# RWKV block with a feed-forward branch: chunks taken in pairs, the up projection by Strassen's algorithm

## What is computed

```python
def attn(x):                      # RWKV v4
    shifted = pad(x, one token)[:, :-1]
    r, k, v = ((mu * x + (1 - mu) * shifted) @ W.T for mu, W in ((mu_r, Wr), (mu_k, Wk), (mu_v, Wv)))
    wkv = wkv_v4(k, v, w, u)      # a recurrence over the tokens: max, exponentials, sums
    return (sigmoid(r) * wkv) @ Wo.T

def ffn(x):
    hidden = silu(x @ W1.T) * (x @ W3.T)       # 2048 wide: the up projection
    return fwht(hidden) @ W2.T                 # Walsh-Hadamard transform, then down

xn = layernorm(x)
out = x + attn(xn) + ffn(xn)
```

## Time and profile before

| | |
|---|---|
| median of 3 runs | 2851.76 us (2851.28 to 2851.79) |
| the profiled execution, its own time | 2851.35 us |
| its span in the trace | 2849.5 us |
| PE, busy share of the span | 99% |
| PEld, busy share | 81% |
| DVE, busy share | 71% |
| ACT, busy share | 32% |
| POOL, busy share | 3% |
| HBM traffic | 191 GB/s over the span |

### The profile page before, as it was taken

How to read it: one execution, slowest core, us unless ns; L and a number is a source line. 1 busy time by engine, 2 the same in 40 slices (tenths; PEclk the granted TensorE clock), 3 DMA queues, 4 the chain that set the end, 5 groups by cost and what they waited for, 6 DMA issues and landing times.

```text
span 2849.5 us, 36275 instructions
## 1 busy us (share of the span) xinstructions
PE 2823.4 (99%) x12352; PEld 2318.1 (81%) x12352; DVE 2014.9 (71%) x2888; ACT 921.1 (32%) x1571; POOL 97.8 (3%) x70
## 2 busy tenths in 40 slices
PE   7999999999999999999999999999999999999999
PEld 4778888888888888888888888888888888888887
DVE  5796767767677775767757677676776767767575
ACT  5444242242322324223242332423224242242321
POOL 0450000000000000000000000000000000000000
PEclk9999999999999999999999999999999999999999
DMA  9777555455555655546455555554545555464554
GB/s 349 248 253 273 185 170 200 163 201 178 185 184 169 207 170 187 193 165 205 162 200 183 174 194 169 191 184 170 200 168 198 178 185 187 165 212 167 172 171 148
DMA packets 168930, 545.97 MB, mean 192 GB/s; under 512 B 20416, under 2 KB 20544, under 8 KB 166464
## 3 DMA queue, kind: packets, MB, share of 16 engines
q1 hardware_dynamic: 168896, 545.53, 56.4%
HBM read 492.97 MB, written 52.49 MB: 191 GB/s over the span
## 4 chain that ended last, share of the span: by engine, by line
PE 96%; DVE 2%; DMA 1%; ACT 0%; issue 0%; POOL 0%; SPq 0%; ACTq 0%; DVEq 0%
PE bank L481 16%; PE bank L483 16%; PE bank L482 16%; PE acc L498 10%; PE acc L497 10%; PE acc L496 10%; PE bank L458 6%; PE bank L457 6%; PE bank L459 6%; PE acc L542 1%; PE acc L519 0%; DMA raw<-units_w 0%; DMA raw<-units_r 0%; DMA fly<-units_w 0%; DVE pab L773 0%; DMA xrow<-x 0%
## 5 line engine op out<-in xcount | busy, mean ns | idle before, releaser
L481 PE MATMUL bank<-xs,ring 128*128 128x512 f32 x1564 | 609.3, 390 | 2.5 <-POOL ring L420 2.4
L483 PE MATMUL bank<-xs,ring 128*128 128x512 f32 x1564 | 608.5, 389 | 0.0
L482 PE MATMUL bank<-xs,ring 128*128 128x512 f32 x1564 | 608.5, 389 | 0.0
L496 PE MATMUL acc<-ring,hid 128*128 128x512 f32 x1024 | 398.4, 389 | 0.4 <-POOL ring L420 0.4
L498 PE MATMUL acc<-ring,hid 128*128 128x512 f32 x1024 | 398.8, 389 | 0.0
L497 PE MATMUL acc<-ring,hid 128*128 128x512 f32 x1024 | 398.3, 389 | 0.0
L859 DVE SCALAR_TENSOR_TENSOR hidf<-hidf,bank 128x512 f32<-128x512 f32 x256 | 175.6, 686 | 284.0 <-ACT hidf L630 284.0
L641 ACT ACTIVATE hid<-hidf 128x512 fp32r<-128x512 f32 x256 | 162.1, 633 | 659.3 <-DVE hidf L862 659.3
L481 PEld LDWEIGHTS bank<-xs,ring 128*128 128x128 f32 x1564 | 293.6, 188 | 65.6 <-DVE hidf L862 3.0
L483 PEld LDWEIGHTS bank<-xs,ring 128*128 128x128 f32 x1564 | 293.6, 188 | 61.0
L482 PEld LDWEIGHTS bank<-xs,ring 128*128 128x128 f32 x1564 | 293.5, 188 | 61.1 <-issue 0.2
(11 more groups left out here) (94 smaller groups left out, 4046.9 us busy)
## 6 DMA issues: line engine op xcount, KB each, us to landing
ring<-split_units SPq DMA_DIRECT2D x780, 512.0 KB, 3.3
split_units<-ring SPq DMA_DIRECT2D x60, 512.0 KB, 4.1
xt<-x_t SPq DMA_DIRECT2D x16, 1024.0 KB, 7.9
res<-x SPq DMA_DIRECT2D x16, 1024.0 KB, 6.4
xrow<-x SPq DMA_DIRECT2D x15, 1024.0 KB, 5.3
out<-res SPq DMA_DIRECT2D x15, 1024.0 KB, 6.0
mix<-token_rows SPq DMA_DIRECT2D x16, 512.0 KB, 4.2
raw<-units_w SPq DMA_DIRECT2D x32, 256.0 KB, 4.6
```

The source lines that it names most:

```text
L481: pe.matmul(banks[b + n][:, :], w[:, 0, col], xs[:, 0, kt, :], start=kt == 0, stop=False)
L482: pe.matmul(banks[b + n][:, :], w[:, 1, col], xs[:, 0, kt, :], start=False, stop=False)
L483: last = pe.matmul(banks[b + n][:, :], w[:, 0, col], xs[:, 1, kt, :], start=False, stop=kt == KT - 1)
L496: pe.matmul(acc[tt][:, :], a[:, 0, col], w[:, 0, :], start=first, stop=False)
```

## The change

Chunks are taken in pairs, 512 tokens (a) and the next 512 (b). For an inner tile the up projection of a pair is a product of 2 x 2 blocks: gate and linear part (W1, W3) by the two halves of the 512 channels, times the two halves of the channels by a and b. Instead of eight block products of 6 matmuls it makes seven (`product`), from sums of the weight halves (`make_sums`, by POOL, once) and sums of the x halves (`right_made` and `right_lo` on DVE, `right_hi` on ACT, once a pair). The seven results are put together in four PSUM banks and in SBUF. ACT copies four intermediate sums out of PSUM in each inner tile (`copy_sum`), and DVE adds three times.

The hidden tiles of a go to the down projection in the same step; PE spreads the four token tiles of one down unit over the seven products. The hidden tiles of b are stored to DRAM (`spilled`), and are loaded again, split and multiplied after the last inner tile (`down_b`), with the k, v and r units of the next pair in turn between them (`r_unit`). No weight unit is resident; W2 and Wo units are loaded twice in a pair.

The recurrence has eight items in a pair (one in the previous down phase, six in the up phase, one after it). Of the five DVE instructions that made the arguments of the exponentials two are left: DVE makes two differences, ACT takes Relu of them and of their negatives, 128 x 1024 each, and then the exponentials, 128 x 1024 each (`rectified`, `exponentials`). Four other DVE instructions of 128 x 512 become two of 128 x 1024.

All units are split by ACT (high) and POOL (low). In the first pair POOL also makes the sums.

```diff
-CHUNKS = B * T // N
+PAIRS = B * T // (2 * N)
+PIECES = (1, 2, 6, 5, 7, 3, 4)
+LEFT_AT = {1: (0, 0), 2: (0, 1), 6: (1, 0), 5: (1, 1), 7: (2, 0), 3: (2, 1), 4: (3, 0)}
+RIGHT = {1: 0, 2: 1, 6: 2, 5: 3, 7: 4, 3: 5, 4: 6}
+WO_AT = {5: 1, 8: 2, 10: 3}
...
+            def make_sums(j):
+                w1, w3 = (raw[RAW_AT[name, j] % RAW] for name in ("w1", "w3"))
+                near, far = slice(0, C // 2), slice(C // 2, C)
+                wait_raw(pool, ("w1", j))
+                wait_raw(pool, ("w3", j))
+                if j == 0:
+                    pool.wait_ge(w2_psum, 2 * FT)
+                else:
+                    pool.wait_ge(split_lo, SPLIT_AT["u", j - 1, 2] + 1)
+                pool.tensor_tensor(sums[:, 1, :], w3[:, near], w3[:, far], ALU.add).then_inc(sum_made, 1)
+                pool.tensor_tensor(sums[:, 2, :], w1[:, near], w3[:, near], ALU.subtract).then_inc(sum_made, 1)
+                pool.wait_ge(sum_made, 4 * j + 1)
+                pool.tensor_tensor(sums[:, 0, :], sums[:, 1, :], w1[:, near], ALU.subtract).then_inc(sum_made, 1)
+                pool.wait_ge(sum_made, 4 * j + 3)
+                pool.tensor_tensor(sums[:, 3, :], w1[:, far], sums[:, 0, :], ALU.subtract).then_inc(sum_made, 1)
...
+            def product(s, j, piece):
+                i, half_unit = LEFT_AT[piece]
+                bank = alpha if piece == 2 else gamma[(j + 2) % 3] if piece in (5, 3) else gamma[j % 3]
+                fresh = piece in (1, 2, 5)
+                w = up_weights(s, j, i)
+                if piece == 1:
+                    if j == 0:
+                        wait(pe, xs_hi, s, 7)
+                        wait(pe, xs_lo, s, 7)
+                        wait(pe, kvr_ready, s, R_UNITS - 3)
+                    elif j == 1:
+                        wait(pe, kvr_ready, s, R_UNITS)
+                    else:
+                        wait(pe, gate_b_sum, s, j - 1)
+                elif piece == 2:
+                    if j == 0:
+                        wait(pe, kvr_ready, s, R_UNITS - 2)
+                    else:
+                        wait(pe, gate_a_sum, s, j)
+                elif piece == 5:
+                    if j == 0:
+                        wait(pe, kvr_ready, s, R_UNITS - 1)
+                    else:
+                        wait(pe, ha_full, s, j)
+                else:
+                    wait(pe, u_copied, s, 4 * j + {6: 1, 7: 2, 3: 3, 4: 4}[piece])
+                for kt in range(2):
+                    at = half_unit * 2 * P + kt * P
+                    col = slice(at, at + P)
+                    high, low = (a[:, RIGHT[piece], kt, :] for a in (xs_high, xs_low))
+                    pe.matmul(bank[:, :], w[:, 0, col], high, start=fresh and kt == 0, stop=False,
+                              skip_group_check=True)
+                    pe.matmul(bank[:, :], w[:, 1, col], high, start=False, stop=False, skip_group_check=True)
+                    last = pe.matmul(bank[:, :], w[:, 0, col], low, start=False, stop=kt == 1,
+                                     skip_group_check=True)
+                last.then_inc(u_done, 1)
...
+            def up_step(s, j):
+                i = SPREAD_AT.get(j)
+                product(s, j, 1)
+                product(s, j, 2)
+                if i is not None:
+                    down_a(s, i, (0,))
+                product(s, j, 6)
+                product(s, j, 5)
+                if i is not None:
+                    down_a(s, i, (1,))
+                product(s, j, 7)
+                product(s, j, 3)
+                if i is not None:
+                    down_a(s, i, (2,))
+                product(s, j, 4)
+                if i is not None:
+                    down_a(s, i, (3,))
+                if j in EXTRA_AT:
+                    down_a(s, EXTRA_AT[j], range(TT))
...
+            def pair(s):
+                for j in range(FT):
+                    up_step(s, j)
+                down_a(s, ND - 2, range(TT))
+                if not is_last(s):
+                    r_unit(s + 1, 0)
+                down_a(s, ND - 1, range(TT))
+                if not is_last(s):
+                    for n in range(1, 4):
+                        r_unit(s + 1, n)
+                for i in range(ND):
+                    down_b(s, i)
+                    if not is_last(s):
+                        r_unit(s + 1, 4 + i)
...
+            def copy_sum(s, j, piece, to):
+                wait(act, u_done, s, 7 * j + PIECES.index(piece) + 1)
+                bank = gamma[(j + 2) % 3] if piece == 5 else gamma[j % 3]
+                act.activation(to, bank[:, :], ACT.Copy).then_inc(u_copied, 1)
+            def rectified(r, w):
+                wait(act, exp_arg, r, 2 * w + 2)
+                act.activation(e_one[:, :, :], z[:, :, :], ACT.Relu).then_inc(wkv_exp, 1)
+                act.activation(e_two[:, :, :], z[:, :, :], ACT.Relu, scale=-1.0).then_inc(wkv_exp, 1)
+            def exponentials(r, w):
+                for i, of in enumerate((e_one, e_two)):
+                    wait(act, wkv_exp, r, 4 * w + i + 1)
+                    act.activation(of[:, :, :], of[:, :, :], ACT.Exp, scale=-1.0).then_inc(wkv_exp, 1)
...
+            def down_step(s, n):
+                with_r, with_d = not is_last(s), not (isinstance(s, int) and s < 0)
+                r = s + 1
+                if with_r:
+                    if n % KT == KT - 1:
+                        evacuate(r, n // KT)
+                    if n + MIX_AHEAD < R_UNITS:
+                        mix_second(r, n + MIX_AHEAD)
+                    if n + MIX_AHEAD + 1 < R_UNITS:
+                        mix_first(r, n + MIX_AHEAD + 1)
+                if with_d:
+                    if 2 <= n < 2 + ND:
+                        hidden_b_hi(s, n - 2)
+                    if n == 1:
+                        rectified(s, 7)
+                        exponentials(s, 7)
+                if with_r:
+                    if n == 11:
+                        rectified(r, 0)
+                        exponentials(r, 0)
+                    if 13 <= n < 20:
+                        right_hi(r, n - 13)
...
+            def gate_a_added(s, j):
+                wait(dve, u_copied, s, 4 * j + 1)
+                wait(dve, u_done, s, 7 * j + 2)
+                dve.tensor_tensor(p_one[j % 2], p_one[j % 2], alpha[:, :], ALU.add).then_inc(gate_a_sum, 1)
+            def gate_a_applied(s, j):
+                wait(dve, tanh_a, s, j + 1)
+                dve.scalar_tensor_tensor(fa[j % 2], fa[j % 2], 1.0, p_one[j % 2], ALU.add,
+                                         ALU.mult).then_inc(gate_a, 1)
+            def gate_b_applied(s, j):
+                wait(dve, tanh_b, s, j + 1)
+                dve.scalar_tensor_tensor(fb, fb, 1.0, u_two[j % 2], ALU.add, ALU.mult).then_inc(gate_b, 1)
+            def hidden_b(s, j):
+                wait(dve, lin_b_sum, s, j + 1)
+                wait(dve, gate_b, s, j + 1)
+                dve.tensor_tensor(fb, fb, u_three, ALU.mult).then_inc(hb_full, 1)
+            def b_added(s, j):
+                wait(dve, u_copied, s, 4 * j + 4)
+                dve.tensor_tensor(u_three, u_three, p_five, ALU.add).then_inc(lin_b_sum, 1)
+                wait(dve, u_done, s, 7 * j + 6)
+                dve.tensor_tensor(u_two[j % 2], u_two[j % 2], gamma[(j + 2) % 3][:, :], ALU.add)\
+                    .then_inc(gate_b_sum, 1)
...
+            def up_step(s, j):
+                if j:
+                    hidden_a(s, j - 1)
+                recurrence(s, j, 0)
+                gate_a_added(s, j)
+                if j:
+                    gate_b_applied(s, j - 1)
+                    hidden_b(s, j - 1)
+                recurrence(s, j, 1)
+                if j:
+                    hidden_a_lo(s, DOWN_A.index(("w2", j - 1)))
+                if j in (0, 4, 7, 9):
+                    hidden_a_lo(s, DOWN_A.index(("wo", (0, 4, 7, 9).index(j))))
+                recurrence(s, j, 2)
+                if not is_last(s):
+                    normalisation(s + 1, j)
+                b_added(s, j)
+                if j in (2, 4, 6, 8) and not is_last(s):
+                    wait(dve, stats_made, s + 1, j)
+                gate_a_applied(s, j)
+                if j in (2, 4, 6, 8) and not is_last(s):
+                    token_mean_var((j - 2) // 4, (j - 2) // 2 % 2)
+            def turn(s):
+                last = is_last(s)
+                if not last:
+                    mix_item(s + 1, 0)
+                hidden_a(s, FT - 1)
+                gate_b_applied(s, FT - 1)
+                if not last:
+                    mix_rest(s + 1, 0)
+                hidden_b(s, FT - 1)
+                hidden_a_lo(s, ND - 1)
+                if not last:
+                    mix_item(s + 1, 1)
+                    mix_item(s + 1, 2)
+                    mix_rest(s + 1, 1)
+                    mix_rest(s + 1, 2)
+                    mix_item(s + 1, 3)
...
+            def down_step(s, n):
```

(25 more changed lines are left out.)

1594 lines of the change are left out of this document (968 added, 626 removed).

## The result

| | median us | range | to the kernel before |
|---|---|---|---|
| before, run beside it | 2851.52 | 2848.70 to 2851.79 | |
| changed | 2912.77 | 2911.22 to 2913.86 | 1.0217, 95% interval 1.0199 to 1.0234 |

The change makes the kernel 61.3 us, 2.2%, slower. The forecast was 2867, slower by 0.5%. The sign was right and the time lies in the range; the loss is four times the one forecast.

The account below looks back on a forecast made before the run. PE was taken as the bound, 99% busy; 768 matmuls fewer save 174.4 us, giving 2675.1. Waits of 4 + 70 + 6 + 7 + 12 + 64 + 23 + 4 make 2865.1, with launch 2867 us; range 2735 to 2945.

Parts of the forecast that it names:

- rival 3: Up products: groups of six matmuls, each with its own wait, run at 0.235 us, not 0.227; 43 us, 2910; chance 0.07.
- the later inner tiles: Up projection of later pairs: DVE at 10.8 of 12.6 us a tile; stalls of 4 us for eight pairs.
- rival 2: Inner tiles of later pairs: DVE bounds every one; 112 us on top, 2975; chance 0.17.
- The hand-over: From inner tiles to down phase: PE waits 8.9 us for b's first down unit, then 1.6; 70 us over seven pairs.
- the half clock: Behind each wait of about 9 us, PE runs at half speed for some time; 1 us each, 7 us in all.
- The last hand-over: Last pair, inner tiles to down units: no next inputs to make, 6 us of waiting.
- Rival 1: Whole kernel: PE stays the bound, first-pair tiles under 14 us, hand-over under 5; 2747 us, faster; chance 0.34.
- Round 11's block: Down phase: ACT's block waits for two DVE differences and delays round 12; 1.7 x 7 = 12 us.
- the down phase: Alternating k/v/r and down units: 5.46 us a round, ACT and DVE fit, one short place; 12 us.
- The first pair's tiles: First pair's inner tiles: DVE, slowed by POOL, bounds them at 16.6 us against PE's 12.6; 64 us.
- The factor of 0.64 us: First pair: each us of POOL's work adds 0.64 us to DVE, read from 39.6 us against 61.9 of POOL's.
- The start: Launch start: more x ahead of W2, later second pass, b's k/v/r units without down units, POOL's sums; 23 us (10 to 40).

## Why the forecast had the sign and not the size

The measured time lies in the stated range, but the loss is four times the forecast's 15 us: the waits sum to 236 us and not 190.

**Right, by the trace and the runs.** The matmuls and their pace: 11584, and 201.5 us for 888 of them, 0.2269 each, so rival 3 falls; the later inner tiles lose nothing, so rival 2 falls too. The hand-over: the same instructions in the same order, 8.3 us of idle time and 2.4 at half clock against 8.9 + 1.6 and 1; the experiments on it moved 72 us, and the wait and the half clock went together. For the half clock 1 us was taken, and the trace has 2.4. The estimate by the Trainium skill ("TensorE: Matmul & The Clock Gate", What's actually happening), whose rule is that an idle array drops to 1.2 GHz and comes back to 2.4 after sustained work, was nearer 2 and came closer. The last hand-over, 5.2 against 6. Rival 1 rested on a hand-over under 5 us and first tiles under 14; they were 8.5 and 16.0. Round 11's block was sized right as well, 1.7 x 7 = 12 us: with the loads on time PE waits 10 us in all for it. In the changed kernel 2.3 of these showed, the rest lay under late loads.

**The step that failed.** "A k/v/r unit and a down unit alternate, 5.46 us a round; ACT needs 2.3 and DVE 1.9 plus a stage": the down phase was checked for the compute engines only, and the sum has 12 us for it and nothing for the last pair's, where 43 and 20 were lost. Three things were left out, and each was run. SP's queue: a moved step issues its loads too, and the load of the down weights stood behind a wait for a group that ends 2.7 us later (23 us). The last pair: its 20 down units were given no line at all in the sum, though with the k/v/r units gone the time that a load has is halved (17 us). The loop, whose body is a pair now: five stops (8 us). Together with b's first unit, 17 us where 7 stood, the down phases were under-sized by 61 us. Against that the first pair and the hand-overs were over-sized.

**Near the size by luck.** The first pair's tiles took 16.0 us against 16.6, but not because DVE bounds them. The factor of 0.64 us of DVE for each of POOL's was misread: the window 1007 to 1151 of the earlier trace rows isn't the inner tiles of a later chunk, it runs over the k/v/r units into the next one. The inner tiles begin at 960.5, and the stretch that answers to 84 to 228 is

```profile
960.50:1104.50 144.00, 144.00 (x635) 118.97 (x634) 109.36 (x157) 38.14 (x65) 1.28 (x1) 1.00 0.53 178
```

That makes 136.3 - 109.4 = 27 us for 61.9 of POOL's, 0.44 for one, and by the prediction's own sum 14.7 us a tile, 34 us and not 64. Here 9.0 x 16 = 144 us of POOL's uncontended work stretched DVE from 170.0 to 224.2, 0.38 for one: read from like stretches, the factor carries over. The 54 us lost have two parts, and the sum had no term for either. PE was idle 38.7 us (255.8 less 217.1); POOL ended 23 of these, DVE and ACT 7 each. And PE was busy 15.6 us longer than in a later pair, 217.1 against 201.5 for the same matmuls, with the granted clock at 0.95 of full, so at half for some 26 us of the stretch, an estimate from that mean. Besides, 5 us of what the first chunk lost before stood in the sum's starting value already. The lines of DVE show where the stretch lies; the first pair, then a later one:

```profile
L1382 DVE TENSOR_TENSOR step<-step 128x512 f32<-128x512 f32 x15 | 17.1, 1143 | 1.9 <-DVE step L1377 0.5
L1363 DVE TENSOR_TENSOR step<-step,gamma 128x512 f32<-128x512 f32 x15 | 10.3, 688 | 1.1
L1324 DVE RECIPROCAL z<-z 128x512 f32<-128x512 f32 x6 | 20.1, 3343 | 0.0
```

```profile
L1382 DVE TENSOR_TENSOR step<-step 128x512 f32<-128x512 f32 x15 | 10.4, 692 | 1.6
L1363 DVE TENSOR_TENSOR step<-step,gamma 128x512 f32<-128x512 f32 x15 | 10.3, 687 | 1.7 <-PE gamma L785 0.6
L1324 DVE RECIPROCAL z<-z 128x512 f32<-128x512 f32 x6 | 20.1, 3346 | 0.0
```

The product of two tiles in SBUF goes from 692 to 1143 ns beside POOL; the one with an operand in PSUM and the reciprocal don't move. The Trainium skill ("SBUF — State Buffer", Who interferes with whom) says that a DVE instruction with two SBUF inputs contends with a GpSimd instruction that reads SBUF, and that one with at most one such input, outside DVE's 2-port modes, does not. For these three lines the trace agrees. Others show that the rule tells who may be held up and not who was: two recurrence instructions with two SBUF inputs kept their length (lines 1328 and 1338, 678 and 682 ns against 685 and 692), and a copy of 128x3, which has one, went from 162 to 778 ns (line 1298).

**The start** was 34 against 23, and again a queue in front of the work was the miss. The second pass and b's k/v/r units came as forecast (7.2 more for 7, 10.1 for 9.4); the first pass, with 2.6 in the sum, lost 13.5 more. There DVE stood before the first half for a semaphore count of the second, and with that moved the pass was 12.5 us shorter, of which 5.6 came back behind it.

## What to carry to other kernels

A change that takes work off the bounding engine has to be checked for every queue, the one that only issues loads included: ask of each load when its slot comes free, what it is issued behind, and how long the consumer then gives it. Look at the last iteration by itself, where the work that covered the others' loads is missing. And when a new order makes an engine wait, look for what merely stands in front: here two edits that move instructions by one and by three steps turned 2.2% slower into 0.4% faster, and three more made it 2% faster.

## What was not expected of the hardware

- A jump of the loop stops PE for 1.9 us with nothing else due (five times), and after some of them the granted clock falls to half for a while, which costs 1.6 us more (once in the changed kernel, after the fourth pair; four times in the run with item 7 later). The kernel before has such a loop too, and loses nothing at it (its excess over the pace, from the first matmul on, stays at 22.8 us from the second chunk to the last). What hides the jump there was not tried.
- An idle time of 8.3 us was followed by 5.3 us of matmuls at half clock (1125.7 to 1131.0), and after a jump's stop of about 2 us half clock followed in some pairs and not in others. In the first pair, whose waits are 6.6 us at most, it cost some 13 us (half of the 26 above).
- DVE's stretch beside POOL depends on where its operands are: 692 to 1143 ns, or none.
